# Two score products moved ahead of a projection in an attention loop that TensorE fills

## What is computed

```
xn = layernorm(x)
q, k, v = rope(xn @ wq), rope(xn @ wk), xn @ wv
attn = softmax(where(allowed, q k^T * sm_scale, neg))     # 4 query heads share one k, v
s = (attn @ v) @ wo
g = silu(w2(silu(w1 xn) * (w3 xn)))
out = x + s * g
```

## Time and profile before

| | |
|---|---|
| median of 3 runs | 802.33 us (802.15 to 803.08) |
| the profiled execution | 802.26 us |
| its span, first to last instruction | 800.4 us |
| PE busy | 796.0 us, 99% |
| DVE, ACT, POOL busy | 567.4, 428.5, 475.2 us |
| granted TensorE clock | 1.00 throughout |

### The profile page before, as it was taken

How to read it: one execution, slowest core, us unless ns; L and a number is a source line. 1 busy time by engine, 2 the same in 40 slices (tenths; PEclk the granted TensorE clock), 3 DMA queues, 4 the chain that set the end, 5 groups by cost and what they waited for, 6 DMA issues and landing times.

```text
span 800.4 us, 13468 instructions
## 1 busy us (share of the span) xinstructions
PE 796.0 (99%) x3966; PEld 672.4 (84%) x3966; DVE 567.4 (71%) x1634; ACT 428.5 (54%) x1104; POOL 475.2 (59%) x357
## 2 busy tenths in 40 slices
PE   9999999999999999999999999999999999999998
PEld 7888888888888888888888888888888888888887
DVE  7715867668448867767686777778677777867785
ACT  5413313223138675666666566666656566665672
POOL 2103314224256774867487486748757674878997
PEclk9999999999999999999999999999999999999999
DMA  9659525201000400400040040004004000420102
GB/s 282 187 178 269 139 67 158 77 29 53 1 27 14 132 14 1 132 2 14 2 131 13 0 131 0 13 0 131 13 0 131 0 13 0 131 66 0 40 0 106
DMA packets 51908, 54.00 MB, mean 67 GB/s; under 512 B 4128, under 2 KB 33184, under 8 KB 51872
## 3 DMA queue, kind: packets, MB, share of 16 engines
q1 hardware_dynamic: 51728, 53.50, 22.6%
q10 hardware_dynamic: 144, 0.07, 0.0%
HBM read 47.25 MB, written 6.29 MB: 67 GB/s over the span
## 4 chain that ended last, share of the span: by engine, by line
PE 93%; POOL 4%; issue 2%; ACT 0%; DVE 0%; POOLq 0%; ACTq 0%
PE bank L1349 26%; PE bank L1350 26%; PE bank L1351 26%; PE bank L1540 3%; PE bank L1556 3%; PE bank L1573 2%; PE bank L1574 2%; PE bank L1575 2%; PE bank L1582 1%; POOL swap L457 1%; PE bank L1579 1%; PE bank L1580 1%; PE bank L1478 1%; POOL acc L488 1%; POOL q L461 1%
## 5 line engine op out<-in xcount | busy, mean ns | idle before, releaser
L457 POOL TENSOR_TENSOR swap<-swap,cst 128x512 f32<-128x512 f32 x80 | 107.9, 1349 | 41.7 <-ACT swap L701 41.7
L722 ACT ACTIVATE probs<-probs,nmx 128x128 f32<-128x128 f32 x256 | 100.0, 392 | 59.9 <-DVE nmx L1123 59.8
L1349 PE MATMUL bank<-xh,wih 128*128 128x512 f32 x320 | 128.9, 403 | 0.0
L1350 PE MATMUL bank<-xl,wih 128*128 128x512 f32 x320 | 125.2, 391 | 0.0
L1351 PE MATMUL bank<-xh,wil 128*128 128x512 f32 x320 | 125.0, 391 | 0.0
L1349 PE MATMUL bank<-woh,oh 128*128 128x512 f32 (+1 forms) x260 | 100.9, 388 | 0.0
L1350 PE MATMUL bank<-wol,oh 128*128 128x512 f32 (+1 forms) x260 | 100.6, 387 | 0.0
L1351 PE MATMUL bank<-woh,ol 128*128 128x512 f32 (+1 forms) x260 | 100.5, 387 | 0.0
L405 POOL TENSOR_TENSOR hl<-act_h,hh 128x512 fp32r<-128x512 f32 x22 | 31.6, 1436 | 99.6 <-ACT hh L603 99.6
L461 POOL TENSOR_TENSOR q<-q,swap 128x512 f32<-128x512 f32 x64 | 86.0, 1344 | 6.6 <-DVE q L1098 1.6
L480 POOL TENSOR_TENSOR ph<-ph,cst 128x512 fp32r<-128x512 f32 x32 | 41.8, 1305 | 73.3 <-ACT ph L737 73.3
(11 more groups left out here) (140 smaller groups left out, 2026.9 us busy)
## 6 DMA issues: line engine op xcount, KB each, us to landing
raw<-in_wq SPq DMA_DIRECT2D x32, 256.0 KB, 4.6
raw<-in_wo SPq DMA_DIRECT2D x32, 256.0 KB, 5.0
pk<-in_w SPq DMA_DIRECT2D x44, 128.0 KB, 3.6
sc<-in_s SPq DMA_DIRECT2D x44, 128.0 KB, 3.8
vals<-stage SPq DMA_DIRECT2D x16, 256.0 KB, 2.8
vraw<-vals SPq DMA_DIRECT2D x16, 256.0 KB, 2.9
pk<-in_w SPq DMA_DIRECT2D x11, 256.0 KB, 2.7
sc<-in_s SPq DMA_DIRECT2D x11, 256.0 KB, 3.1
```

The source lines that it names most:

```text
L457: nc.gpsimd.tensor_tensor(v, v, spread(sin.unsqueeze(1), P, 2, SEQ), ALU.mult).then_inc(sin_done, 1)
L722: e = nc.scalar.activation(probs[:, s, c0:c1], probs[:, s, c0:c1], ACT.Exp, bias=nmx[:, s, i:i + 1], scale=-1.0, accum_out=rsum[:, s, i:i ...
L1349: nc.tensor.matmul(out_, sh, mh, start=(i == 0), stop=False)
L1350: nc.tensor.matmul(out_, sh, ml, start=False, stop=False)
```

## The change

Three lists are reordered, and nothing is added or taken away. TensorE issues the score products of heads 0 and 1 of the second batch right behind the transposes and ahead of projection 0. ScalarE takes the exponentials of these two heads ahead of the swap of projection 0 (and of the fourth `hi_wo` and `v_hi`). VectorE masks them ahead of the cosine product of projection 0. GpSimd's and SyncE's lists stay. It acts in the 14 steps (0, 1) to (7, 0).

```
@@ ScalarE, step @@
                 if w:
                     for h in range(3):
                         hi_wo(g, h)
+                exps(g, bp, 1, 0)
+                exps(g, bp, 1, 1)
                 halves(ng, nbp, 0)
                 if w:
                     hi_wo(g, 3)
                 v_hi(ng, nbp)
-                exps(g, bp, 1, 0)
-                exps(g, bp, 1, 1)
                 halves(ng, nbp, 1)
@@ VectorE, step @@
                 if bp == 0:
                     first_wo_lo(g)
+                masking(g, bp, 1, 0)
                 cos_part(ng, nbp, 0)
-                masking(g, bp, 1, 0)
                 v_lo(ng, nbp)
@@ TensorE, step @@
-                project(ng, nbp, 0)
                 scores(g, bp, 1, 0)
                 scores(g, bp, 1, 1)
+                project(ng, nbp, 0)
                 project(ng, nbp, 1)
```

## The result

The changed kernel takes 811.34 us (median of 5 runs, 811.08 to 811.94) against 802.33 us (also a median of 5, 802.15 to 803.08). The ratio is 1.0113, with a 95% interval of 1.0102 to 1.0125: slower by 1.1%. The forecast was 812.0 us, with a range of 807 to 815.5. All times here are of executions at the full granted clock; one execution of the run with TensorE's list put back, the one that was profiled, had a granted clock of 0.71 and took 1058.74 us, and its trace is not used. The execution profiled after has a span of 809.3 us, 8.9 more than before.

The account below looks back on a forecast made before the run. TensorE was taken as the bound, without gaps in usual steps, with GpSimd's slack thinnest. Losses of 8.6 us (six steps) and 1.5 (step (7, 0)) less 0.3 give 9.8 on 802.26: 812.0 us, range 807 to 815.5.

Parts of the forecast that it names:

- TensorE has no gap to give back: TensorE in usual steps of 35.1 us: no wait to take away, so the time can only rise.
- the saved change of operand type: TensorE, one change from plain fp32 to fp32r operands fewer: gain of 0.02 us a step, 0.3 us over 14.
- The start of GpSimd's list: GpSimd's first sine product, steps with bp = 0: starts at 398.18 in step (2, 0), 2.32 us late.
- The length of the list: GpSimd, first sine product to end of low masked copy: 18.72 us without gaps, bounds 18.16 and 19.2.
- The sum: Whole kernel: 1.43 us lost in each of six steps, 1.47 in step (7, 0), less 0.3: 9.8 us.
- Steps with bp = 1 at nothing: Seven steps with bp = 1: swap of projection 0 about 1.15 us later, covered by 0.3 us; costed at nothing.
- that 1.45 us would be absorbed: GpSimd, steps with bp = 0: idle stretches of 0.57 and 0.67 plus 0.21 us slack absorb a late first sine product.
- the low bound of 0.87 us: Matmul behind L1582, steps with bp = 0: least loss per step, with GpSimd's list at 18.16 us.
- the rival of the short list: GpSimd's list keeps its short 18.16 us, stretches falling as before: 6.4 us lost, 808.6 us; chance 0.22.
- the distance of 0.87 us to a full absorption: First sine product's lateness beyond 1.45 us; rival that GpSimd absorbs all, not slower: 802.0 us, chance 0.07.
- The rival of more collisions: GpSimd and VectorE meet more often, or VectorE late too: 0.45 us more in seven steps, 815.2 us; chance 0.13.

Follow-up runs that it names:

- the first run: The changed kernel with ScalarE's list put back (swap of projection 0, fourth `hi_wo` and `v_hi` ahead of both heads' exponentials): 805.75 us, ratio 1.0041.
- half dose: The changed kernel with only head 0's exponentials ahead of the swap of projection 0, head 1's behind `v_hi`: 806.15 us, ratio 1.0045.

## Why the prediction was right, point by point

*TensorE has no gap to give back.* Right. In the steps with bp = 1 the new order is worth some 0.02 us (35.107 us on average, against 35.124), as I took it; that the saved change of operand type is the reason was not tested alone. But I counted it in 14 steps, and in the seven with bp = 0 GpSimd sets the time and nothing of it can show: 0.1 us, not 0.3.

*The start of GpSimd's list.* I had 7.48 us behind the transposes (398.18 - 390.70), measured 7.41. All of the pieces were right within 0.07 us: masking behind `first_wo_lo`, 0.86 us to the exponentials (395.29 to 396.15), 1.68 over them, 1.28 from swap to sine product.

*The length of the list.* 18.72 taken, 18.70 measured. The row of step (7, 0) was the right one to carry over. The reason given is borne out: in step (2, 0) before, two single operations of the list stand at 1.6 us or more, and after it three, with two more at 1.46 and 1.47 where they were 1.29 and 1.35; and of two products alike but for one input, only the one with both inputs in SBUF lengthens it. The Trainium skill (SBUF — State Buffer, "Who interferes with whom") says that such an instruction and a GpSimd instruction that reads SBUF exclude each other. The trace agrees: one meeting cost GpSimd 0.45 us and VectorE 0.51. That GpSimd is held up for the whole of VectorE's instruction the trace doesn't show: the product's other form takes 0.69 us, more than GpSimd lost.

*The sum.* 1.43 us a step forecast, 1.3 measured; 1.47 forecast for step (7, 0), 1.38 measured. The term is too large by the 0.07 us of the start, nearly all of it from taking the end of `wol`'s record where the next operation starts 0.07 sooner, and by the 0.02 of the list. 10.05 - 0.3 was forecast and 9.3 - 0.1 lost.

*Steps with bp = 1 at nothing.* Right; the swap ended 1.22 us later (at 6.23 us in the step, before 5.01) and the sine product started at 6.61 as before (6.60).

*What was wrong, though the forecast didn't rest on it: that 1.45 us would be absorbed.* I added GpSimd's two idle stretches to its slack, as if they were its own. They end when ScalarE delivers, and for one of them, ahead of sine product 3, ScalarE can be late by the same route. In the first run VectorE starts masking heads 2 and 3 at 15.86 us in the step in place of 14.81: 0.62 us of that because swap 1 came later, and 0.42 because the probabilities' product was stretched to 1.30 us from 0.88 beside GpSimd. Swap 3 comes 1.06 late with it, and the idle stretch stays. The larger part is the other half: where the idle stretches do close, the gapless list is 18.7 us and not 18.2. With 18.72 the sine product may start at 25.17 - 0.40 - 18.72 = 6.05 us, 0.89 us later than before, not 1.45. A delay of 1.17 us already costs 0.4 a step (first run) and 1.47 costs 0.58 (half dose). In the sum the 1.45 was not used, since it adds the gapless list to the start; there the passage and the sum contradict each other. What rested on it are the low bound of 0.87 us, the rival of the short list and the distance of 0.87 us to a full absorption. By the measured start that distance was 2.25 - 0.89 = 1.36 us. That rival deserved less than the chance it had.

*The rival of the short list* (808.6 us) fell to the same finding: in step (2, 0) of the changed kernel and of the five runs that have the full list on a late start without a gap and nothing put beside it that meets GpSimd, it measured 18.69 to 18.76 us. *The rival of more collisions* (815.2 us) is what the extra product with two SBUF inputs made by hand, 814.5 us; the changed kernel's list is no longer than that of step (7, 0) before, so it had none beyond those.

Still open is how step (0, 1) of the first run splits its 1.1 us between its causes, the table load that comes later and the key's low part, which VectorE makes in 1.78 us ahead of the masking; moving the latter took all of it away.

## What to carry to other kernels

In a kernel whose main engine has no gap, moving work ahead has next to nothing to win; here it won 0.1 us and lost 9.3. Price it at the slack of the engine that is served next in line, by reading who is queued behind the moved work. Don't count an engine's idle stretches as slack before you have asked who ends them, and take the length of a list from a place where it runs without a gap, since operations that exclude each other can meet more often there. Where such a list is the limit, taking one operation off it can buy back most of a late start: here 7.35 of 9.0 us, with the start as late as before.

## What the runs showed of the hardware that I had not expected

A late operand costs TensorE more than the lateness of that one matmul: L1582 starts 0.06 us after the copy's end, but the next one only 0.34 us later in place of 0.23. The prediction had this from step (7, 0) before, and it came out the same in step (2, 0) after. ScalarE's change of activation table between Silu and Exp takes 1.28 us, and what stands in front of it decides when it comes: in step (0, 1) of the changed kernel it falls into idle time, and behind the late swap of the first run it ended 1.17 us later than before. What it cost there stays open. Whether an input of a 128x512 product on VectorE lies in PSUM or in SBUF was worth 3.1 us of this kernel's time over seven steps, through GpSimd.
